# Two transformer layers on one core: fourth-chunk queries, gates, modulation, rows and three value blocks move from beside the first unit's maxima to beside the second unit's first eight score tiles

## What is computed

```
mod = (_silu(L0_c) @ L0_wmod).reshape(L0_c.shape[0], 6, 1, -1)
sa, ca, ga, sb, cb, gb = (mod[:, 0], mod[:, 1], mod[:, 2], mod[:, 3], mod[:, 4], mod[:, 5])
ga = (2 * (ga >= 0) - 1) * jnp.maximum(jnp.abs(ga), 0.25)
h = _layernorm(x, axis=-1) * (1 + ca) + sa
q = (x @ Wq.T + bq).reshape(b, s, NHEADS, DK)      # 16 heads of 8, of h
k = (x @ Wk.T + bk).reshape(b, s, NHEADS, DK)
v = (x @ Wv.T + bv).reshape(b, s, NHEADS, DV)
w = jnp.einsum('bshd,bzhd->bhsz', q, k)
w = jax.nn.softmax(w / jnp.sqrt(jnp.float32(DV)), axis=-1)
vw = jnp.einsum('bhsz,bzhd->bshd', w, v)
x = x + ga * (vw.reshape(b, s, NHEADS * DV) @ Wo.T + bo)
```

## Time and profile before

| what | value |
|---|---|
| median of three runs | 1112.59 us (1110.43 to 1114.13) |
| the profiled execution's own time | 1107.93 us |
| its span | 1106.1 us |
| mean granted clock of TensorE | 0.967 |

### The profile page before, as it was taken

The page is one execution under the profiler, slowest core; times in us unless marked ns, Lnnn a source line. Parts: engine busy times, 40 slices in busy tenths (PEclk is TensorE's granted clock), DMA queues, the critical chain, the costliest instruction groups (busy, mean ns, idle before and its releaser), DMA issues.

```text
span 1106.1 us, 22247 instructions
## 1 busy us (share of the span) xinstructions
PE 1017.8 (92%) x8770; PEld 351.0 (32%) x8770; DVE 897.3 (81%) x1135; ACT 820.1 (74%) x1585; POOL 170.1 (15%) x308
## 2 busy tenths in 40 slices
PE   4879999999999999999998999799988998899997
PEld 2332222222222222222232344233344563333324
DVE  5999999999999999999988777556677767797603
ACT  3229999998999988999976677366754665656785
POOL 4533200003000012000034000411022003000101
PEclk9569999999999999999999999999999999999997
DMA  3460511000000000000003331115100431200000
GB/s 108 122 157 2 142 33 19 13 2 2 2 2 2 3 1 2 2 2 2 2 1 110 111 107 30 39 31 93 25 2 13 142 97 34 36 10 2 1 11 10
DMA packets 47693, 42.06 MB, mean 38 GB/s; under 512 B 6534, under 2 KB 45798, under 8 KB 47590
## 3 DMA queue, kind: packets, MB, share of 16 engines
q1 hardware_dynamic: 45190, 35.17, 12.9%
q0 software_dynamic: 1824, 5.25, 1.7%
q10 hardware_dynamic: 576, 0.23, 0.1%
HBM read 26.83 MB, written 13.30 MB: 36 GB/s over the span
## 4 chain that ended last, share of the span: by engine, by line
PE 71%; DVE 10%; ACT 8%; issue 4%; SPq 2%; DMA 2%; POOL 1%; another core or an unknown queue 1%; POOLq 0%; ACTq 0%; DVEq 0%
PE O L949 26%; PE T L920 14%; PE S L879 8%; DVE mx L1217 5%; ACT PT L1463 5%; PE S L886 5%; PE T L929 4%; PE S L1060 2%; PE S L1028 2%; SPq L1833 1%; PE T L1068 1%; PE S L1018 1%; ACT PT L1457 1%; PE T L958 1%; PE S L929 1%
## 5 line engine op out<-in xcount | busy, mean ns | idle before, releaser
L1217 DVE TENSOR_REDUCE mx<-S 128x2 f32<-128x1024 f32 (+2 forms) x672 | 759.4, 1179 | 75.0 <-PE S L879 27.1
L1463 ACT ACTIVATE PT<-T 128x512 f32<-128x512 f32 (+2 forms) x1280 | 675.7, 580 | 107.9 <-PE T L920 34.6
L949 PE MATMUL O<-PT,Va 128*9 128x256 f32 (+1 forms) x4032 | 317.5, 387 | 3.3 <-ACT Os L1498 3.3
L879 PE MATMUL S<-Ks,Qs 48*128 48x512 bf16 x1024 | 205.7, 395 | 17.3 <-DVE mx L1217 9.9
L920 PE MATMUL T<-Qs,Ks 51*128 51x512 bf16 x1024 | 201.7, 386 | 11.8 <-ACT PT L1463 8.1
L920 PEld LDWEIGHTS T<-Qs,Ks 51*128 51x128 bf16 x1024 | 55.9, 93 | 222.7 <-issue 124.7
L949 PEld LDWEIGHTS O<-PT,Va 128*9 128x9 f32 x4032 | 59.8, 88 | 206.8 <-issue 197.2
L886 PE MATMUL S<-K,Qs 96*128 96x512 bf16 (+3 forms) x320 | 90.1, 351 | 3.7 <-DVE mx L1217 3.3
L929 PE MATMUL T<-Qs,K 99*128 99x512 bf16 (+3 forms) x256 | 71.3, 346 | 13.9 <-ACT PT L1463 8.0
L949 PE MATMUL O<-PT,V 128*17 128x512 f32 (+3 forms) x640 | 74.4, 537 | 0.0
L1718 POOL CAST n<-nm 128x16 bf16<-128x16 f32 x24 | 5.5, 228 | 391.6 <-DVE nm L1225 391.3
(11 more groups left out here) (284 smaller groups left out, 835.0 us busy)
## 6 DMA issues: line engine op xcount, KB each, us to landing
Qs<-in_L_ffn_experts SPq DMA_DIRECT2D x28, 192.0 KB, 2.6
Ks<-in_L_ffn_experts SPq DMA_DIRECT2D x20, 192.0 KB, 2.6
Vf<-sorted_x SPq DMA_DIRECT2D x12, 256.0 KB, 4.5
sorted_y<-Vf SPq DMA_DIRECT2D x12, 256.0 KB, 2.3
Qs<-rows_q SPq DMA_DIRECT2D x24, 128.0 KB, 4.7
rows_q<-q SPq DMA_DIRECT2D x7, 384.0 KB, 3.1
Qs<-rows_q SPq DMA_DIRECT2D x36, 64.0 KB
sorted_x<-XP POOLq DMA_DIRECT2D x1, 1792.0 KB, 10.7
```

What stands on the lines that cost most here:

```text
L879: m = e.matmul(two[:, i, :], Qs[r0:r0 + 48, hp, q0:q0 + 128], Ks[r0:r0 + 48, hp, CH * kb:CH * kb + CH], start=True, stop=True, tile_positi ...
L949: m = e.matmul(Ob[32 * g:32 * g + d1, lo:hi], v, PT[(2 * j + g // 2) % 4][:, p0 + lo:p0 + hi], start=(kt == 0 and halves[0] == 0), stop=Tr ...
L1217: e.tensor_reduce(mx[:, u % 2, h0:h0 + 2, kb], two[:, :, 0:n], AX.X, ALU.max).then_inc(free, 1)
L1463: e.activation(PT[(2 * j + pair) % 4][:, CH * i + lo:CH * i + CH], bank[:, lo:CH], ACT.Exp).then_inc(free, 1)
```

## The change

Unit 0's 32 tiles keep only the first four halves of query projections (chunks 1 and 2), and the value block of chunk 0 (now after the 30th tile). The last three second-part loads of keys are placed after the 14th tile and no longer behind the store of the fourth chunk's queries. The fourth chunk's two query halves, the gates, the value blocks of chunks 1 to 3, the six modulation columns and the rows stand between the first tiles of unit 1, of which eight and not seven come before the first step. The entry of `LEAD` for unit 1 goes from 5 to 3.

```
-LEAD = {(L, u): 5 if L == 0 or u == 7 else 4 if u > 4 else 3 for L, n in ((0, 16), (1, 8)) for u in range(n)}
+LEAD = {(L, u): 3 if (L, u) == (0, 1) else 5 if L == 0 or u == 7 else 4 if u > 4 else 3 for L, n in ((0, 16), (1, 8)) for u in range(n)}
...
-        elif i in (5, 7, 9, 11, 13, 15):
+        elif i in (5, 7, 9, 11):
             project_q(1 + (i - 5) // 4, (i - 5) // 2 % 2)
...
             elif i == 11:
                 load_rest(1)
-            elif i == 15:
-                load_rest(3)
-        elif i == 18:
-            beside("mod", 1)
-        elif i == 20:
-            beside("gates")
-        elif i == 22:
-            beside("rows")
-        elif i in (25, 27, 29, 31):
-            values((i - 25) // 2)
-    for i in range(7):
+        elif i == 13:
+            load_rest(3)
+        elif i == 29:
+            values(0)
+
+    beside_shifts = {3: [lambda: project_q(3, 1)],
+                     4: [lambda: beside("gates"), lambda: P.stage("gate_values")],
+                     5: [lambda: values(1)],
+                     6: [lambda: beside("mod", 1), lambda: values(2)],
+                     7: [lambda: beside("rows"), lambda: values(3)]}
+    for i in range(8):
         if i == 2:
+            project_q(3, 0)
             urgent.pop(0)[1]()
-            P.stage("gate_values")
             P.stage("late_loads")
+        for fn in beside_shifts.get(i, ()):
+            fn()
         emit_s()
```

## The result

The changed kernel took 1116.04 us (median of 20 runs, 1112.09 to 1120.39) against 1111.05 us before (20 runs, 1107.31 to 1114.66). The ratio is 1.0043 with a 95% interval of 1.003 to 1.0055: about 4.8 us slower. The forecast was +0.5 us, 1113.1, and most likely no change that a measurement can tell; the loss is larger than the 3.3 us that I had named for that. The stated range, 1109.3 to 1118.0, holds the measured time. The nearest case is the rival in which the clock stays low: its +5.6 us is 0.8 from the measured +4.8, while its 1118.2 is 2.2 above, since the three runs that I started from had a median 1.5 us above that of the 20. One profiled execution of the changed kernel took 1116.90 us, its span is 1115.2 us.

The account below looks back on a forecast made before the run. DVE and PE together pace layer 0; PE's one-time blocks make DVE's gaps in the head. Gains of 2.8 and 1.8 us against +5.1 between single tiles give +0.5 us: 1112.59 becomes 1113.1, range 1109.3 to 1118.0.

Parts of the forecast that it names:

- the rival in which the clock stays low: PE at the low clock up to unit 1's first step: unit 1's negated maxima at 112.6, +5.6 us, 1118.2; chance 0.20.
- Unit 0's maxima: DVE gaps of 1.63, 0.57 and 0.62 us go, gaining 2.8 us; unit 0's negated maxima at 65.2, not 68.05.
- the kept gap: DVE's 0.99 us gap in unit 0, behind the one value block left there at the low clock, was to stay.
- My own sign of being wrong: Wrong if unit 1's negated maxima (the mark) come before 104 or after 110, or stay while the end moves.
- PE sets the new stretch: In unit 1's first eight tiles PE needs 17.8 us at low clock, 9.8 at high; DVE 6.9 for six tiles.
- When the clock rises: 6 to 9 us after PE becomes dense at 65.2; first step at 78.4 to 79.8.
- Key loads at no price: The last 18 key loads go ahead of the last queries' store; unit 1's seventh tile no longer waits for them.
- The steps behind it: First five half steps take 5.9 us, not 9.1, so the sixth stands at 84.3 against 84.12; DVE gains 1.8 us.
- The four gaps of before: DVE gaps of 0.38, 0.71, 0.30 and 0.42 us in steps PE ran at low clock; to go, 1.8 us.
- The modulation at the high clock: In unit 1's first tiles, twelve f32 weight loads with one output column each take 1.5 us, estimated between 1.35 and 2.7.
- The sum: -2.8 us before unit 0's negated maxima, -1.8 in the steps, +5.1 between single tiles: +0.5 us, 1113.1.
- the end moves by what the mark moves by: The list is unchanged from unit 0's second step on, so a shift of unit 1's negated maxima shifts the end equally.

Follow-up runs that it names:

- e11: The changed kernel with each of the six modulation matmuls issued twice into the same column; 1118.00 us, ratio 1.0054 to the kernel before.
- e3: The changed kernel with the value blocks of chunks 1 to 3 put back beside unit 0; 1110.17 us, ratio 0.9998 to the kernel before.
- e9: The changed kernel with the value blocks of chunks 1 to 3 moved beside unit 0's steps 2, 5 and 8; 1113.74 us, ratio 1.0033 to the kernel before.
- e4: The changed kernel with the store of the third chunk's queries issued behind the last 18 key loads; 1116.02 us, ratio 1.0052 to the kernel before.
- e1: The changed kernel with a bf16 filler matmul of ones behind each of unit 0's tiles 13 to 29; 1113.89 us, ratio 1.0036 to the kernel before.
- e5: The changed kernel with an f32 filler of real data behind each of unit 0's tiles 13 to 29; 1116.99 us, ratio 1.0031 to the kernel before.

## Why the prediction was right or wrong

- **Unit 0's maxima: right.** Forecast 65.2, measured 65.00; the kept gap is 0.99 to the digit, and PE stayed hidden. The clock was not at 0.50 throughout, as I had it from 26 to 71: it was high from 29.1 to 32.8, hence 0.57 from 26 to 50.
- **My own sign of being wrong came.** I had named a mark after 110; it came at 114.71.
- **PE sets the new stretch: right.** The low-clock sum was 17.8 us for two query halves, turn, gates, values, modulation, rows and six tiles. From 65.56 to the end of the eighth tile at 84.38 it took 18.8, with 1.3 of waiting for keys; e11 showed the price up to the first step as one for one.
- **When the clock rises: wrong, and this is the step that failed.** I took 6 to 9 us of dense work from two stretches of before. PE was dense from 68.6 on and the clock rose only at about 84, 15 us later. The first step came at 84.79, where I had 78.4 to 79.8 for the forecast and 84.0 for the rival in which the clock stays low. I gave that rival 0.20. Even more cases of the kernel before would not have warned me: there is one more, in which PE worked without a gap from 46.9 and the clock rose at about 53.5, again after 6 to 7 us:

```profile
50.00:56.50 6.50, 5.28 (x25) 2.92 (x25) 5.63 (x9) 1.04 (x3) 0.00 (x0) 0.73 0.67 164
```

What spoke against a rise that follows from dense work was 26 to 50 us, with PE busy for 21.49 of 24.00 at 0.50. So the rise of the clock in one order of work did not carry over to another.
- **Key loads at no price: wrong, but small in time.** I looked at the seventh tile's wait only. The third tile, now 2.3 us earlier, waited 1.29 us. With the same order of loads this wait is 2.00 us in e3 and absent in e9 and e11, so it differs from execution to execution, and e4 won nothing in time.
- **The steps behind it: half right.** The four gaps of before were to go; the changed kernel has gaps of 0.71, 0.38 and smaller again, for its clock, high at 84.1 to 87.5 (0.96), fell once more (0.55 from 87.5 to 91.0). From the first step to the mark it took 29.9 us, where I had 28.7.
- **The modulation at the high clock: right.** I took 1.5 as an estimate; e4 has 1.50 for the twelve matmuls against 2.72 at the low level. By the Trainium skill, page "TensorE: Matmul & The Clock Gate", section "LDWEIGHTS (loading the stationary operand)", a weight load has one time for its number of columns, with no term for the clock. The trace does not agree for these f32 loads: one is listed with 333 ns in e3 and 192 ns in e9.
- **The sum.** Forecast +0.5 for the mark, the rival's +5.6; measured +7.7 in the profile (114.71 against 106.97), 1.3 of which is the key wait. The low-clock rival's mark, 112.6, is short by 2.1: 0.8 up to the first step, where the wait for keys is 1.3, and 1.3 in the steps. In the runs the change is +4.8: the two profiles compared are single executions. That the end moves by what the mark moves by did not hold from profile to profile: the spans differ by 9.1 us, the marks by 7.7, and over all 14 profiles the rest behind the mark takes 999.1 to 1007.3 us.
- **What was luck.** That the range holds the measured time is due to the rival with a chance of 0.20, whose price set its upper end, and not to the forecast.

## What to carry to other kernels

When an engine is the bound with a gap of the other engines beside it (here DVE at 1.18 us a tile and PE at 0.61), that gap is where one-time work belongs, even if it makes a few gaps: the blocks that were moved out, 14 us of PE at their low-clock lengths, had cost 2.8 us of gaps there. With them between eight tiles, the way from unit 0's negated maxima to unit 1's grew by 10.8 us (38.9 before, 49.7 after), 1.3 of it the wait for keys. And price a block of PE at both clock levels: take its low-clock time until a profile of this very order of work shows the clock high. Last, compare two kernels by many runs: here single executions of one kernel lie up to 8.3 us apart, more than the change.

## What the runs showed of the hardware

- PE can be busy all the time and stay at the low level. It was busy for 13.55 of 13.70 us at 0.51 in the changed kernel, and in e1 and e5 for 21 us without a gap at 0.50, with fillers of bf16 and of f32. What made the clock rise in some stretches and not in these, the runs do not show.
- Within one kernel, 20 runs spread over 8.3 us, and their time goes with the time at the low clock (0.38 us for each us). Over 14 profiles of kernels with the same list behind the mark, that part shows the same slope, 0.39.
- The same 12 weight loads and matmuls of 128x128 f32 took 2.72 us at the low level and 1.50 at the high one.
- The DVE operation behind the copies of the modulation (L1131, two instructions) took 0.62 us and not 0.23; it took 0.99 in e11 and 0.23 in e3 and e5, and 0.23 in every profile in which it stands beside unit 0. The cause was not tried.
